# Two graph-attention layers on edge lists: selections on GpSimd, layer two's transposed selections made ahead, x added by GpSimd and the row sum on ScalarE

## The reference

```
# layer one
scores = einsum('hnd,hmd->hnm', x * 32**-0.5, x2)
attn   = softmax(where(adj > 0, scores, -9e15), axis=-1)
x      = layernorm(x + attn @ v)
# layer two
h      = x @ W_w.T + W_b
e      = leaky_relu(s_src[:, None, :] + s_dst[None, :, :], 0.2)   # s_src = h . a_src, s_dst = h . a_dst
attn   = softmax(where(adj == 0, -1e9, e), axis=1)
x      = layernorm(x + elu(attn @ h))
```

## Time and profile before

| | us |
|---|---|
| median of 3 runs | 475.83 |
| lowest and highest run | 473.26 and 477.1 |
| profiled execution, its own time | 475.88 |
| span of the profile (first to last instruction) | 472.7 |

### The profile page before, as it was taken

One profiled execution on the slowest core, in us unless ns is written; L12 is line 12 of the kernel. 1 busy time (PEld: TensorE's weight loads), 2 busy tenths in 40 slices (PEclk: granted clock), 3 DMA queues, 4 the chain that ended last, 5 costly groups with the idle time before them and its releaser, 6 DMA issues.

```text
span 472.7 us, 5744 instructions
## 1 busy us (share of the span) xinstructions
PE 259.2 (55%) x1490; PEld 184.4 (39%) x1490; DVE 294.7 (62%) x822; ACT 180.9 (38%) x448; POOL 249.1 (53%) x409
## 2 busy tenths in 40 slices
PE   0327767738653874788686873330102727385870
PEld 0216545526342653555465552220001615164550
DVE  3996989998987898898956510300013326477771
ACT  6423755424732762345341442000020025547553
POOL 7367364578368587477872237777750746100000
PEclk9957857677776987597977888575555757677795
DMA  8968276557458335152232002444440433201001
GB/s 307 300 199 316 96 259 194 182 147 253 149 166 281 102 126 147 60 143 79 77 88 72 12 23 83 109 112 112 107 105 0 109 81 96 67 22 47 10 13 49
DMA packets 24516, 57.94 MB, mean 123 GB/s; under 512 B 6592, under 2 KB 14912, under 8 KB 22432
## 3 DMA queue, kind: packets, MB, share of 16 engines
q0 software_dynamic: 10032, 31.77, 24.2%
q1 hardware_dynamic: 14448, 25.77, 15.5%
HBM read 53.20 MB, written 4.33 MB: 122 GB/s over the span
## 4 chain that ended last, share of the span: by engine, by line
PE 25%; issue 19%; DVE 18%; POOL 11%; another core or an unknown queue 10%; ACT 8%; SPq 4%; DMA 2%; DVEq 1%; ACTq 0%; POOLq 0%
PE e_po L1355 11%; POOL e_ring L974 4%; PE e_pj L1372 3%; DVE e_weighted L1609 3%; PE e_pq L1299 3%; DVE e_raw L1424 3%; PE e_pj L1281 2%; DMA e_adj<-in_adj 1%; DVE e_score L1557 1%; ACT e_sel_edges L1133 1%; SPq L900 1%; POOL e_h_sum L1053 1%; ACT e_vals L1077 1%; DVE e_prod L1553 1%
## 5 line engine op out<-in xcount | busy, mean ns | idle before, releaser
L1355 PE MATMUL e_po<-e_weighted,e_sel_edges 128*128 128x264 f32 x312 | 98.7, 475 | 8.0 <-DVE e_weighted L1609 5.0
L974 POOL DMA_INDIRECT e_ring<-table,e_col_i x78 | 74.6, 957 | 44.0 <-issue 21.6
L974 POOL DMA_INDIRECT e_ring<-in_kv,e_col_i x78 | 79.2, 1016 | 34.1 <-issue 20.8
L1355 PEld LDWEIGHTS e_po<-e_weighted,e_sel_edges 128*128 128x128 f32 x312 | 72.4, 240 | 28.1 <-DVE e_weighted L1609 8.3
L1133 ACT COPY e_sel_edges<-e_pt 128x512 f32<-128x512 f32 (+3 forms) x45 | 23.6, 523 | 59.8 <-issue 32.8
L1339 PE MATMUL e_po<-e_mean_row,e_diagonal 128*128 128x264 f32 x64 | 23.1, 450 | 41.0 <-issue 23.2
L1299 PE MATMUL e_pq<-e_parts,e_sel_rows 128*128 128x256 bf16 x234 | 42.7, 347 | 1.2 <-DVE e_prod L1553 0.9
L1424 DVE MAX8 e_raw<-e_vals 128x8 bf16<-128x256 bf16 (+1 forms) x88 | 41.5, 513 | 1.0
L1609 DVE TENSOR_TENSOR e_weighted<-e_ring,e_pc 128x528 f32<-128x528 f32 (+1 forms) x55 | 35.7, 683 | 9.2 <-PE e_po L1355 7.6
L1264 PE MATMUL e_pt<-e_identb,e_sel_rows 128*128 128x128 bf16 x156 | 18.8, 246 | 34.3 <-ACT e_sel_edges L1133 17.0
L1393 DVE RECIPROCAL e_rden<-e_po 128x8 f32<-128x8 f32 x32 | 6.5, 204 | 48.6 <-remote 36.6
(11 more groups left out here) (197 smaller groups left out, 543.4 us busy)
## 6 DMA issues: line engine op xcount, KB each, us to landing
e_adj<-in_adj SPq DMA_DIRECT2D x16, 1024.0 KB
table<-e_hx SPq DMA_DIRECT2D x16, 136.0 KB
e_ring<-in_kv SPq DMA_DIRECT2D x1, 2112.0 KB, 13.3
out<-e_prod SPq DMA_DIRECT2D x16, 128.0 KB
e_ring<-in_kv,e_col_i POOLq DMA_INDIRECT x78
e_ring<-table,e_col_i POOLq DMA_INDIRECT x78
e_xres<-in_x SPq DMA_DIRECT2D x2, 512.0 KB, 9.1
e_xres<-in_x SPq DMA_DIRECT2D x3, 256.0 KB, 10.0
```

The lines of the kernel that those rows point to most:

```text
L974: nc.gpsimd.indirect_dma_start(out=rings[layer][:, q % RING[layer], :], out_offset=None, in_=kv if layer == 0 else table, in_offset=bass.I ...
L1355: nc.tensor.matmul(po[n % 2][:, 0:CV], sel_edges[:, (layer * plan.n_chunks + q) % TURNED, :], weighted[:, b % 3, j * CV:(j + 1) * CV], sta ...
```

## The change

1. **Selections.** The stage "select" is issued by GpSimd in place of VectorE (17 instructions over 78 chunks).
2. **Layer two's turned selections.** They no longer share the 24 places: 64 of the 78 chunks get a place in `search`, memory that the search in adj (`adj_tile`, `vals`, `far`) has used up to then, and the last 14 go to `sel_edges` after layer one's sums. Stages "turn_edges"/"copy_edges" of layer two get rank 80 and come after the last ones of layer one.
3. **bf16 parts.** `upper(ap)` reads the upper two bytes of each f32 as bf16. ScalarE's two copies per group (L1107, L1112) go; GpSimd still subtracts.
4. **Layer one's residual.** "norm" only divides. GpSimd adds x (stage "add_x"). ScalarE takes the row sum by a Copy with an accumulator, in place of L1162.
5. **Mean of h.** "copy_norm" is two copies with accumulators; VectorE adds the sums ("column_sums"), TensorE multiplies them by the weights ("mean_h"). GpSimd's `h_sum` goes.
6. **Spread.** "evac" writes h and the scores by two instructions, and "spread" is two instructions per group in place of five per tile.
7. **Buffers and reports.** `diagonal` has three buffers. TensorE reports sums by `sums_done`: per batch in layer one, about every eighth chunk and at the end of a tile in layer two. `weighted` has three places in layer one and ten in layer two.

```diff
-            put("DVE", 0.115 * m + 0.05, rank, ("select", k, i, c, m), ("far", k, i, c, m))
+            put("POOL", 0.3 * m + 0.2, rank, ("select", k, i, c, m), ("far", k, i, c, m))
...
-            put("DVE", 1.35, rank - 0.2, ("norm", k), end, ("x", plan.group_of_k(k)), ("normed", k - 4) if k >= 4 else None)
-            put("ACT", 1.0, rank - 0.3, ("spread_of", k), ("norm", k), ("project", k - 2) if k >= 2 else None)
+            put("DVE", 0.75, rank - 0.2, ("norm", k), end, ("normed", k - 4) if k >= 4 else None)
+            put("POOL", 0.75, rank - 0.3, ("add_x", k), ("norm", k), ("x", plan.group_of_k(k)))
+            put("ACT", 1.4, rank - 0.3, ("spread_of", k), ("add_x", k), ("project", k - 2) if k >= 2 else None)
...
+    for q, m in plan.quads_ahead:
+        free = ("weigh",) + where[len(where) // 2 - 1] if q + m > PLACES_AHEAD else None
+        put("PE", 0.1 * m + 0.15, 80, ("turn_edges", 1, q, m), ("move", NG - 1), last_rows(NK - 1), free, ("turn_edges", 0) + plan.quads[NG - 1][-1], holds="pt")
+        put("ACT", 0.13 * m + 0.1, 80, ("copy_edges", 1, q, m), ("turn_edges", 1, q, m), ("sums",) + where[len(where) // 2 - 1] if free else None, frees="pt")
...
+                    self.reports.append(layer == 0 or c % 8 == 6 or any(c < e <= c + m for e in ends))
...
+        def upper(ap):
+
+            return ap.bitcast(BF16).rearrange("p k (c e) -> p k c e", e=2)[:, :, :, 1]
...
+                elif stage[0] == "select":
+                    _, k, i, c0, n = stage
+                    q = plan.first[plan.order[k]] + c0
+                    pool.wait_ge(s("far_ready"), i + 1)
+                    nc.gpsimd.tensor_scalar(sel_rows[:, q * P:(q + n) * P], far[:, i % 2, 0:n * P], half[:, k:k + 1], None, ALU.is_le).then_inc(s("sel_ready"), 1)
...
+                elif stage[0] == "add_x":
+                    k = stage[1]
+                    pool.wait_ge(s("sums_read"), k + 1)
+                    pool.wait_ge(x_loaded[plan.group_of_k(k)], 16)
+                    nc.gpsimd.tensor_tensor(y[:, k % 4, :], y[:, k % 4, :], xres[:, k, :], ALU.add).then_inc(s("z_ready"), 1)
...
-                    own.did(nc.scalar.activation(neg_mean[:, one], total[:, one], ACT.Copy, scale=-1.0 / C))
+                    own.did(nc.scalar.activation(xts[k % 2][:], y[:, k % 4, :], ACT.Copy, scale=-1.0 / C, accum_out=neg_mean[:, one]))
...
-                    if b >= 3:
-                        dve.wait_ge(s("chunk_summed"), plan.summed_by(b - 3))
-                    v.tensor_tensor(weighted[:, b % 3, 0:m * CV].rearrange("p (c h d) -> p c h d", c=m, d=D1), rings[layer][:, at:at + m, lo:lo + CV].rearrange("p c (h d) -> p c h d", d=D1),
+                    had = plan.place_before(b)
+                    if had is not None:
+                        dve.wait_ge(s("sums_done"), plan.reports_by(had))
```

232 lines of the change are left out of this document (122 added, 110 removed).

## The result

The changed kernel took 478.76 us (median of 12 runs, 474.25 to 481.52), the kernel before 477.04 us beside it (473.26 to 478.6). The ratio is 1.0089, with a 95% interval of 1.0046 to 1.0133.

What follows compares the result with a forecast made beforehand. No engine bounds the kernel throughout: VectorE mostly binds layer one to 250 us, and late TensorE reports during gathers stall layer two's start. 475.9 - 11 + 4 - 7 = 461.9, taken as 462 us; 8-in-10 range 440 to 488.

Steps and rivals of the forecast that it cites:

- Part 1: Layer one, up to the first table gather: moving work off VectorE saves 11 us, ends -16 and +3.
- two or so tiles follow one another: 2 us: End of layer one, 250 to 287 us: each tile's chain some 1 us longer, costing 2 us.
- at nothing under VectorE's cover: Layer one: ScalarE loses copies, gains about as much by a second pass at half load; priced at zero.
- -16 for VectorE's freed work, +3 for the lock: First 250 us, taken as VectorE-bound: 16 us saved, 3 us lost as GpSimd and VectorE hold one another up.
- rival 3: GpSimd binds layer one; slow selections, locks and delayed gathers give back all its gain: 473 us, chance 0.18.
- The pair in rows 6: Layer one: a 2.15 us VectorE selection beside a 1.16 us GpSimd operation, read as agreeing with an exclusive port lock.
- Part 2: Start of layer two, first gather to group 1's first weighing: 4 us later, ends -35 and +15.
- Rival 2: Start of layer two: turns ahead of group 0's scores get caught in the slow time; 482 us, chance 0.26.
- the fifth of the nine turns: Start of layer two: if about this turn isn't copied 8 us after the first gather, the slower case holds.
- about one report gets through per gather: Start of layer two: TensorE gets through about once per gather, 1.2 us per instruction against 1.25 us between gathers.
- Rival 1: Start of layer two: fewer semaphore raises dissolve the stall, group 1 weighed at 38 us; about 424 us, chance 0.12.
- Part 3: Rest of layer two: ten places remove waits, ScalarE's copies go; 7 us saved, ends -2 and -12.

Runs made afterwards that it cites:

- e5: Changed kernel with the selections issued by VectorE again, every stage kept at its place in the order; 473.87 us, ratio 0.9972.
- e6: Changed kernel with selections and added x both back on VectorE, its order kept; 469.0 us, ratio 0.9890.
- e9: Changed kernel with only x added by VectorE (row sum with it), selections still on GpSimd, order kept; 468.8 us, ratio 0.9900.
- e10: e6 with GpSimd pauses of 0.96 us behind every second gather of layer two; 452.0 us, ratio 0.9503.
- e11: e6 with tiny pauses (0.12 us) behind every second gather of layer two; 480.36 us, ratio 1.0120.
- e3: Changed kernel with selections and added x both back on VectorE, planner free to order anew; 471.4 us, ratio 0.9847.
- e7: e3 with long GpSimd pauses behind every second gather of layer two; 457.09 us, ratio 0.9651.
- e8: e3 with the selections of group 1 and later turned only after group 0's last sum; 477.95 us, ratio 1.0069.
- e18: Changed kernel unedited, run again beside the kernel before; 477.14 us against 474.69, ratio 0.9957.
- e4: Changed kernel with layer two's gathers halted at chunk 24 until group 1's first two chunks were weighed; 483.31 us, ratio 1.0177.
- e12: Kernel before the change, with only pauses of 0.96 us behind every second gather of layer two added; 459.25 us, ratio 0.9690.
- e16: e9 with three weighted places in layer two instead of ten and sums reported every batch; 413.07 us beside 421.41 before, ratio 0.9748.
- e1: Changed kernel with the selections issued by VectorE again, planner free to order anew; 484.25 us, ratio 1.0204.
- e2: Changed kernel with x added by VectorE again (row sum with it), planner free to order anew; 475.73 us, ratio 1.0005.
- e13: e9 with pauses of 0.96 us behind every second gather of layer two; 452.39 us beside 421.41 before, ratio 1.0654.
- e15: e9 with long pauses behind only every fourth gather of layer two; 433.77 us beside 421.41 before, ratio 1.0268.
- e17: Changed kernel as it is, with pauses of 0.96 us behind every second gather of layer two; 456.07 us, ratio 0.9607.

## Why the prediction was wrong

**Part 1 (-11 us, measured -0.9; with other profiles of the same layer one between -2.7 and +1.7) is the step that failed.** Two of its terms were wrong, and the rest of the change, which it put at nothing, moved layer one as much.

The term "two or so tiles follow one another: 2 us" for the added x on GpSimd. It costed the longer chain at the tail of layer one alone. The square of e5, e6 and e9 puts the added x, with ScalarE's longer pass, at 8 us of the first gather (4 to 5 us by the medians), and the timelines show 4.9 of them between the tenth and the fourteenth division: the added x waits behind gathers, ScalarE waits for it with other groups' copies behind, and TensorE with other groups' turns. The prediction had said in so many words that "a tile's chain waits for the gathers ahead of them", and then gave that no price; it had cost ScalarE "at nothing under VectorE's cover". Without this one move the number for layer one would have come near, but by luck: e9 has its first gather at 276.0 us, 10.9 us before, and the mean with its four companions is 278.4. It isn't VectorE's freed work that gives this, for with all of it back on VectorE (e6, e10, e11) the first gather comes at 278.5 as well, 8 us before the kernel before. About 7 of these are the order, as e3, e7 and e8 with the same work and the planner's own order come at 284.9 to 286.3.

The term "-16 for VectorE's freed work, +3 for the lock". It held VectorE to bound the first 250 us, so that each microsecond off it would show. VectorE got half of its work back over the span and 3.9 us of it in the first 250. The selections cost GpSimd 29.9 us, not 21 (the upper bound from L1053's 3.2 ns per column was the nearest), and VectorE's own instructions grew by 7 to 8 us. None of it shows in the first gather: with the order kept the selections are worth nothing on either engine, and 11 us more work of VectorE don't delay layer one. That is rival 3's claim for this half of the part; its figure for the whole (473) was nearer than the forecast, though its cause, that GpSimd binds, isn't borne out either, as 29.9 us off GpSimd move nothing. The pair in rows 6 shows VectorE lengthened, but it had started 0.57 us before GpSimd's operation and ended 0.42 us behind it, so it doesn't show a lock held by whoever starts first.

**Part 2 (+4 us, measured +4.8, and +1.8 in e18) held in size by luck.** The forecast had one unbroken run of 52 gathers and group 1's weighing 12.4 + 4 us behind it. What came was another path: group 0 is weighed 43 us late, so the ring stops the run after 44 gathers, at 55.0 us; 6.4 us of halt, 8 gathers in 9.7 us and 11.0 us to the weighing of group 1 make 82.1 us. Rival 2 was nearer to it: group 0 at 62 us (60.4 measured) and the second run behind it. But its reason was not what happened. By its own sign, the fifth of the nine turns copied or not 8 us after the first gather, it stood on the edge: that copy ran promptly from 7.6 to 8.2 us. Seven were copied by 296.9 us, and group 0's scores were turned at 300.64, 14.6 us after the first gather and not when the gathers stop. Late were the reports of group 0's own steps, as shown above. Its consequence held in kind, since group 1's scores stand behind group 0's division in VectorE's list, and was oversized: 21.7 us from one weighing to the other, where it had 30. In e8 the forecast's own picture comes true, with group 0 early and one run of 52 gathers, and group 1 is weighed at 81.2 us.

The reading under both, that reports of TensorE are late while gathers run without a pause, is shown by e4, e7, e10 and e12 for the condition in which they ran; e16 shows that such a run of gathers isn't enough by itself. That about one report gets through per gather, the prediction's finer reading, was not tested. Rival 1 (fewer reports dissolve the stall) is refuted by the changed kernel itself, which reports sums every eighth chunk and stalls as before.

**Part 3 (-7 us, measured -1.5).** In the eight profiles of the changed kernel and its variants with late reports and the turns ahead (after, e1, e2, e3, e5, e6, e9, e18: 103.0 to 107.7) the mean is 105.0, so about -3.4 us against 108.4, near the small end of the range given (-2 to -12). The waits for the sums of three batches back are gone from the weighings, but the last gather comes 111 to 116 us after the first in all of them, hardly sooner than before (116.8), and of the stretch behind it there is little that ten places could shorten. What places, reports and turns each give stays open.

**The larger lever lay outside the change.** 0.96 us of pause after every second gather takes 3.1% off the kernel before (e12). The forecast and its rivals took the gathers' pace as given.

**What stays open.** Why e13 to e16 and the kernel before beside them ran without late reports: the gathers' issue (1.25 us each) and the granted clock (0.73 to 0.75 in the mean) are as in the others, and the record names the same chip for them as for e9 to e12. One thing in the profiles does tell them apart. Of the stores and gathers of layer two, e16's view of DMAs gives the time from issue to landing (the last number, us), as those of e13 to e15 do; in all the other profiles too few landings are recorded to give one, in e10 too, whose pauses leave no report of layer two late:

```profile
table<-e_hx SPq DMA_DIRECT2D x16, 136.0 KB, 1.8
e_ring<-table,e_col_i POOLq DMA_INDIRECT x78, 2.9
```

```profile
table<-e_hx SPq DMA_DIRECT2D x16, 136.0 KB
e_ring<-table,e_col_i POOLq DMA_INDIRECT x78
```

So the two conditions differ in what the profiler records of semaphores through the whole kernel, and not only where reports are late. Every timed execution on record comes with a span and a granted clock, as a profiled one does, so whether reports would be late without the profiler no run shows. Open too are how short a pause may be, which of the turns make group 0 late, and what places, reports and turns are worth one by one.

## What to carry to other kernels

A step moved to an engine whose list is full of long fixed-cost instructions has to be priced by where it stands in that list and by what is queued behind each of its waiters, not by the engine's free share: here 16 additions of 0.8 us, with a longer pass on ScalarE behind each, put the first gather 8 us back, although GpSimd was idle for a third of layer one. To compare an engine against another, keep the order and change only who issues: with a planner that orders anew the selections' way back read +11 us, and with the order kept 0 (e1, e5). And if one engine's finished work reaches the others late while another issues DMAs back to back, try pauses in the issuing, and measure them in both conditions: here they gave 3% in the one and cost in the other.

## What the runs showed of the hardware

- While GpSimd issues indirect gathers back to back (one each 1.25 us), TensorE's semaphore reports can arrive late, by up to 32 us (finished at 313.1, read at 344.87 in the kernel before); those of VectorE and ScalarE don't (at 300.27 and 306.77 us in the changed kernel TensorE starts 0.14 us behind ScalarE's end and 0.05 behind VectorE's). The first late one is finished 11.6 us after the first gather in the changed kernel, and 24.0 us in the kernel before, whose TensorE has few instructions until then. With a pause of 0.96 us after every second gather none of layer two is late (e7, e10, e12, e17); with 0.12 us they are (e11).
- It is a condition that can be absent: beside e13 to e16 the kernel before took 421.41 us (420.37 to 423.5, 11 runs), 11% less. There the pauses only cost: 39 us the long ones (452.39 against e16's 413.07), 19 us the half ones (431.88), though e16 also has other places and reports. With late reports the long ones gave 15 to 17 us (e12: 473.92 to 459.25; e10 against e6: 469.0 to 452.0).
- A compare with a value per partition on GpSimd (f32 in, bf16 out) takes 1247 ns for 384 and 2913 ns for 1024 columns, 3.9 times VectorE's 752 ns for 1024, and stretches VectorE's short instructions beside it from 0.3 to 1.3 and 1.7 us.
